# Two set-up blocks of a graph kernel made one: the destination list loaded by ScalarE's queue, the table clears begun behind the source keys with a semaphore for each table, and the index lists and three groups' loads moved beside the input stage

## The reference, cut to what matters

```python
xn = _layernorm(x, axis=-1)
# layer 0, twice (the edges come sorted by dst):
msg = ew[:, None] * h[src]
agg = jax.ops.segment_sum(msg, dst, num_segments=x.shape[0])
# layer 1:
edge_proj = edge_attr @ W_sum + b_sum
sum3d = jax.ops.segment_sum(edge_proj, src, num_segments=num_nodes)
```

## Time and profile before

| | us |
|---|---|
| median of 3 runs | 6724.04 (6717.91 to 6748.71) |
| the profiled execution | 6726.44 |
| its span in the trace | 6724.7 |
| mean granted TensorE clock | 0.735 of full speed |
| GpSimd busy, by the page | 4268.7 (63%) |

### The profile page before, as it was taken

How to read it: one execution, slowest core, us unless ns; L and a number is a source line. 1 busy time by engine, 2 the same in 40 slices (tenths; PEclk the granted TensorE clock), 3 DMA queues, 4 the chain that set the end, 5 groups by cost and what they waited for, 6 DMA issues and landing times. The chain is left out here.

```text
span 6724.7 us, 77268 instructions
## 1 busy us (share of the span) xinstructions
PE 3884.2 (58%) x19263; PEld 3286.8 (49%) x19263; DVE 2787.9 (41%) x7801; ACT 2353.9 (35%) x6709; POOL 4268.7 (63%) x3891
## 2 busy tenths in 40 slices
PE   4655555555555555555655229977765645655653
PEld 3555555545445555554444128866544434444442
DVE  5544444444414444444478666535640011101125
ACT  1225555555435555555433113333421111111112
POOL 3886666666676666666678757875546666666632
PEclk8666666676776766777767569989877777777776
DMA  7774232233473332323478637867341111211235
GB/s 208 133 142 141 86 87 86 86 87 86 87 138 86 87 87 85 87 86 87 85 140 164 174 101 160 168 137 214 107 115 28 32 27 43 45 29 43 45 102 177
DMA packets 691306, 690.18 MB, mean 103 GB/s; under 512 B 97322, under 2 KB 609156, under 8 KB 690360
## 3 DMA queue, kind: packets, MB, share of 16 engines
q0 software_dynamic: 244480, 323.25, 23.8%
q1 hardware_dynamic: 433016, 339.78, 16.6%
q10 hardware_dynamic: 13632, 25.14, 1.0%
HBM read 484.11 MB, written 203.71 MB: 102 GB/s over the span
## 5 line engine op out<-in xcount | busy, mean ns | idle before, releaser
L625 POOL DMA_INDIRECT a_msg<-h_d,a_idx x1664 | 1577.9, 948 | 962.4 <-issue 414.1
L671 PE MATMUL a_part<-a_pick,a_msg 128*128 128x128 f32 x6656 | 1351.0, 369 | 1123.7 <-issue 609.5
L671 PEld LDWEIGHTS a_part<-a_pick,a_msg 128*128 128x128 f32 x6656 | 1218.8, 273 | 1241.9 <-issue 1213.8
L397 POOL DMA_INDIRECT sums_d<-ss_total,ss_row_i x784 | 1287.8, 1643 | 423.5 <-issue 282.6
L3413 POOL DMA_INDIRECT es_edge<-gat_rows_d,el_idx x1024 | 986.4, 963 | 490.2 <-issue 288.3
L651 DVE TENSOR_TENSOR acc<-acc,a_part 128x256 f32 x1664 | 700.9, 421 | 1330.8 <-remote 615.3
L2405 PE MATMUL e_yp<-cb_lent 128*128 128x256 f32 (+1 forms) x1568 | 484.1, 462 | 460.9 <-ACTq L2369 259.9
L2405 PEld LDWEIGHTS e_yp<-cb_lent 128*128 128x128 f32 (+1 forms) x1568 | 363.7, 236 | 584.4 <-ACTq L2369 309.8
L2347 DVE TENSOR_TENSOR cb_lent<-e_yp,cb_lent 128x512 f32<-128x512 f32 (+1 forms) x100 | 68.1, 681 | 1361.6 <-DMA y_d<-mg_y 1016.6
L638 DVE TENSOR_SCALAR a_pick<-ramp,conv_rel,conv_weight 128x128 f32<-128x128 f32 x1680 | 589.5, 352 | 101.5 <-issue 73.5
L2367 ACT ACTIVATE cb_lent<-e_hp,e_b1c 128x256 f32<-128x256 f32 (+1 forms) x400 | 155.3, 471 | 1228.7 <-DMA gm_zo<-in_L_gnn_z_out,gm_out_i 995.8
(11 more groups left out here) (517 smaller groups left out, 5884.7 us busy)
## 6 DMA issues: line engine op xcount, KB each, us to landing
ss_key_row<-keys_d SPq DMA_DIRECT2D x98, 512.0 KB
ss_pay<-in_edge_attr SPq DMA_DIRECT2D x97, 512.0 KB
a_msg<-h_d,a_idx POOLq DMA_INDIRECT x1664
experts_d<-cb_lent SPq DMA_DIRECT2D x96, 256.0 KB
es_edge<-gat_rows_d,el_idx POOLq DMA_INDIRECT x1024
cb_lent<-experts_d SPq DMA_DIRECT2D x29, 512.0 KB
y_rows_d<-node_h SPq DMA_DIRECT2D x28, 512.0 KB
e_xs<-y_rows_d SPq DMA_DIRECT2D x56, 256.0 KB
```

What stands on the lines that cost most here:

```text
L397: nc.gpsimd.indirect_dma_start(self.out_d[q], bass.IndirectOffsetOnAxis(ap=self.row_i[n % 4][:, j:j + 1], axis=0), self.total[n % 4][:, j, ...
L625: nc.gpsimd.indirect_dma_start(msg[(h % 2) * K + b][:], None, table, bass.IndirectOffsetOnAxis(ap=idx[h][:, b:b + 1], axis=0)).then_inc(ga ...
L671: mm = nc.tensor.matmul(part[b % BANKS][:, half, :], msg[(h % 2) * K + b][:, half * P:(half + 1) * P], pick[b][:], start=True, stop=True)
```

## The change

`edge_keys` and `conv_steps` are replaced by one class, `EdgeOrder`, whose parts are called from two places.

- `EdgeOrder.set_up` is one block. The destinations are loaded by ScalarE's queue (`load(act, 1)`), source and weights by SyncE's. ScalarE issues the first SET_UP_CLEARS = 14 of the 24 clears once the source keys have been stored. The input stage's parameters are issued here (`StageParams.issue`) and are waited for in the input stage. `sums.set_up` stands behind the copies of the turned keys. Two groups are loaded instead of five; the first is summed and its rows are chosen.
- `input_stage` takes the rest: four clears ahead of ScalarE's first round and two after each of its first three phases; the seven gathers ahead of GpSimd's scatters; key rows and payload of groups 2 to 4 and the far lists behind the first four x; one gathered block a round in rounds 1 to 7 (`make_rel`, `turn`, `copy_out`); the digit lists and the words in rounds 8 to 10.
- `cleared` is one semaphore for each table, and the first scatter to a table waits for the six clears of that table alone.

```diff
+            def load(eng, j):
+                eng.wait_ge(padded, j + 1)
+                eng.dma_start(raw[j][0:full, :], ...).then_inc(loaded[j], 16)
...
+            @block.sync
+            def _(sp):
+                load(sp, 0)
+                load(sp, 2)
+                for j in (0, 1):
+                    sp.wait_ge(made, j + 1)
+                    sp.dma_start(keys_d[:, j, :]...).then_inc(self.stored[j], 16)
+                sp.wait_ge(loaded[2], 32)
+                sp.dma_start(keys_d[:, 2, :]...).then_inc(self.stored[2], 16)
+                sp.wait_ge(none_made, 1)
+                sp.dma_start(self.sort.sorted_d[0:1, :], self.none[:]).then_inc(none_stored, 16)
+                params.issue(sp)
+                sp.wait_ge(self.stored[0], 16)
+                for n in (0, 1):
+                    sums.load(sp, n, n)
+                sp.wait_ge(none_stored, 16)
+
+            @block.scalar
+            def _(act):
+                load(act, 1)
+                act.wait_ge(zeroed, 1)
+                act.wait_ge(self.stored[0], 16)
+                self.clear(act, 0, SET_UP_CLEARS)
+                for half in (0, 1):
+                    sums.evict_half(act, 0, 0, half)
...
@@ EdgeSums.scatter
-            if chunk == 0:
-                pool.wait_ge(self.cleared, 16 * CLEARS * Q)
+            if nth == 0:
+                pool.wait_ge(self.cleared[q], 16 * CLEARS)
...
@@ input_stage, VectorE
-                    if phase == 2 + i:
+                    if phase == 2 + i and g > first:
                         sums.choose_rows(dve, g - 1, g - 1)
+                if phase == 0 and 1 <= n <= NSB:
+                    order.make_rel(dve, n - 1)
+                if phase == 3 and 1 <= n <= NSB:
+                    order.copy_out(dve, n - 1)
+                if (n, phase) == (8, 3):
+                    order.list_dst_digits(dve)
+                if (n, phase) == (9, 3):
+                    order.list_far_digits(dve)
+                if (n, phase) == (10, 3):
+                    order.make_words(dve)
...
@@ input_stage, GpSimd, TensorE, ScalarE
+            order.gather(pool)
             sums.scatter(pool, first - 2, first + IN_GROUPS - 2)
...
+                if phase == 1 and 1 <= n <= NSB:
+                    order.turn(pe, n - 1)
...
+                if n == 0 and phase < 3:
+                    order.clear(act, SET_UP_CLEARS + 4 + 2 * phase, SET_UP_CLEARS + 6 + 2 * phase)
+            order.clear(act, SET_UP_CLEARS, SET_UP_CLEARS + 4)
             over_fours(act, first_root, copy, head_root, relu, beside=serve)
```

More of the change, by code:

```diff
@@ L123, in _, with __init__, issue, wait @@
             nc.vector.tensor_copy(ramp_16[:], ramp_i[:].unsqueeze(2).broadcast_to([P, P, 16]))
[L126 to L138, removed]
+class StageParams:
+    def __init__(self, k, ctx, tag, loads):
+        self.tiles = [ctx.enter_context(k.nc.sbuf_tensor(f"{tag}_{name}", shape, F32)) for name, shape, _ in loads]
+        self.sources = [source for _, _, source in loads]
+        self.loaded = ctx.enter_context(k.semaphore(f"{tag}_params_in"))
+    def issue(self, sp):
+        for t, source in zip(self.tiles, self.sources):
+            sp.dma_start(t[:], source, allow_slow_non_contiguous=True).then_inc(self.loaded, 16)
+    def wait(self, eng):
+        eng.wait_ge(self.loaded, 16 * len(self.tiles))
@@ L139, in sb @@
         def sb(name, shape, dt=F32):
-            return c.enter_context(nc.sbuf_tensor(f"ek_{name}", shape, dt))
+            return c.enter_context(nc.sbuf_tensor(f"eo_{name}", shape, dt))
         def sem(name):
[L143 to L202, removed]
+            return c.enter_context(k.semaphore(f"eo_{name}"))
@@ new lines, in __init__, with bank @@
+        self.first, self.chunk_i = sb("first", [P, NSB]), sb("chunk_i", [P, NSB], I32)
+        self.got = [sb(f"got{b}", [P, 3 * P]) for b in range(NSB)]
+        self.far_in, self.index_made, self.rel_made, self.turned_to, self.copied = map(sem, (
+            "far_in", "index_made", "rel_made", "turned_to", "copied"))
+        self.stored = [sem(f"stored{j}") for j in range(3)]
+        self.gathered = [sem(f"gathered{b}") for b in range(NSB)]
+    def bank(self, c):
+        self.turned = c.enter_context(self.nc.psum_tensor("eo_turned", [P, 4, P], F32))
@@ new lines, in clear, with gather @@
+    def clear(self, act, first, last):
+        run = self.tables[0].shape[0] * self.tables[0].shape[1] // P // CLEARS
+        zero = self.spare.rearrange("p t f -> p (t f)")[:, 0:run]
+        for n in range(first, last):
+            q, part = divmod(n, CLEARS)
+            rows = self.tables[q].rearrange("(p r) f -> p (r f)", p=P)
+            act.dma_start(rows[:, part * run:(part + 1) * run], zero).then_inc(self.cleared[q], 16)
+    def gather(self, pool):
+        table = self.keys_d.rearrange("c j e -> c (j e)")
+        pool.wait_ge(self.index_made, 1)
+        for j in range(3):
+            pool.wait_ge(self.stored[j], 16)
+        for b in range(NSB):
+            self.nc.gpsimd.indirect_dma_start(self.got[b][:], None, table, bass.IndirectOffsetOnAxis(
+                ap=self.chunk_i[:, b:b + 1], axis=0)).then_inc(self.gathered[b], 16)
@@ L1165, in serve @@
                     sums.load(sp, g + 4, g + 4)
-            over_fours_io(sp, load, store, beside=serve)
+            over_fours_io(sp, load, store, beside=serve, behind=order.load_rest)
             all_stored(sp, h_out)
@@ L1352 @@
 CLEARS = 6
+SET_UP_CLEARS = 14
 EARLY_GROUPS = 1
```

356 lines of the change are left out of this document (199 added, 157 removed).

## The result

The changed kernel took 6709.62 us (median of 20 runs, 6693.14 to 6723.36); in the same comparison the kernel before took 6731.96 (20 runs, 6710.90 to 6750.53). The ratio is 0.9969, with an interval of 0.9959 to 0.9980: about 21 us faster, by 14 to 28. The interval lies clear of 1, but the gain is less than half a per cent, so by the bound of the prediction it counts as no change, where "faster" had 0.68. 6709.62 lies 4 us above the range. The profiled execution has a span of 6716.3 us; that of before had 6724.7.

What follows compares the result with a forecast made beforehand. GpSimd's train of scatters was taken to bound the input stage, with a wait-bound set-up ahead of it. Starting the fourth scatter at 86 instead of 126.91 gave 6726.4 - 41 = 6685.4, less 2.4 to the median: 6683 us, range 6660 to 6706.

Steps and rivals of the forecast that it cites:

- step 6: Input stage, last table: head roots end 80.5, issues 81.2, clears land after 5 us; fourth scatter waits from 74 to 86.
- step 7: Scatters after the fourth: it starts 41 us earlier, next rows come in time, 1.96 us a scatter, no more waits than before.
- everything later hangs on that: Stages after the input stage: its end fixes all that follows, so the 41 us gain reaches the program's end.
- step 1: Set-up, list loads: both queues share three DMA engines at 68 GB/s; source and destinations both there at about 18.6, weights 24.3.
- steps 2 and 3: Set-up: VectorE's sums.set_up done at 32.4, step index 36.9; clears start at 26 and run until about 50.
- step 4: First group: key rows end at 51 beside the clears, last eviction 57.3, input stage starts at about 59, bounds 50 and 68.
- step 5: Gathers at the head of GpSimd's input block: 9.5 us, unhidden; first scatter at 68.5 instead of 120.44, at most 52 us gained.
- Step 8: Work moved into the input stage costs nothing: 12.5 us spare a four, under 2.5 us added on VectorE.
- the start is later: Rival, chance 0.22: first key rows and x sit longer behind clears, or second x is late; gain 26 down to 12.
- GpSimd is the only limit: Rival, chance 0.20: clears end sooner or ScalarE's land before 74; gain 52 us, 6664 to 6675.
- does nothing: Rival, chance 0.04: something other than the train of scatters sets the input stage's end; 6724.
- slower: Rival, chance 0.04: the input stage's first ten rounds become the bound as VectorE waits; 37.6 us a four gives 6758.

Runs made afterwards that it cites:

- rows16: Changed kernel with each 111-row list loaded as 96 and 15 rows; 6635.51 us, ratio 0.9921 to the kernel before.
- dst_sp: Changed kernel with the destinations back on SyncE's queue, between source and weights; one execution, 5964.22 us, aggregate stage at 452.99.
- rest_late: Changed kernel with group 4's loads behind the second x and the far lists in round 3; aggregate stage at 457.55 us.
- after_again: Changed kernel, unedited, compared again with the kernel before on chip B; 6658.87 us, ratio 0.9953.
- after_third: Changed kernel, unedited, compared with the kernel before on chip C; 5968.67 us, ratio 0.9941.
- after_fifth: Changed kernel, unedited, compared with the kernel before on chip D; 6658.56 us, ratio 0.9955.
- rows16_again: Repeat on chip D of the changed kernel with lists loaded as 96 and 15 rows; 6635.52 us, ratio 0.9929 to the kernel before.
- rows16_loads: rows16 with sums.set_up behind the casts, loads of groups 0 and 1 ahead of the parameters, clears behind the second payload; 5962.61 us, ratio 0.9929.
- evict_split: rows16_loads with the first group's sums copied after ten of ScalarE's fourteen clears, the other four behind; 6641.33 us, ratio 0.9938.
- delay35: Changed kernel with an idle block of 34 memsets on VectorE between input stage and first aggregate; 6702.86 us, ratio 1.0021 to the kernel before.
- last_first: Changed kernel with all ten remaining clears issued at the head of the input stage; fourth scatter 6.6 us earlier, aggregate stage at 450.95 us.

## Why the prediction was right and wrong

The forecast was a gain of 41 us; measured were 21 by the ratio, 22 by the medians. Three terms make the difference: step 6 (4.0 us), step 7 (2.4), and "everything later hangs on that" (12 to 14).

1. *The lists, step 1.* That both queues use three engines is shown, by rows16, dst_sp and the share of 0.19. What failed is "both at 18.6": the casts at 15.91 and 21.73 lie either side of it, since the destinations' packets began 4 us after their issue. The two queues' shares were even from then on, and the three engines moved 80 GB/s from 11 to 15 us where 68 was taken. The first clear, which hangs on the store of the source keys, was not changed by it.
2. *VectorE and the first clear, steps 2 and 3.* First clear at 25.00, forecast 26. VectorE ran behind by the late destinations: sums.set_up ended at 34.9, forecast 32.4.
3. *The first group, step 4.* Key rows at 51.04, forecast 51; last copy at 57.57, forecast 57.3 for its end; x at 59.12, forecast 59. The first is partly luck: the key rows were asked for 2.5 us late (34.92) and landed in 16.1 us, not 18.6. SyncE's queue had 47 GB/s beside the clears from 41 to 49 us (0.38 MB), not 37.
4. *The gathers, step 5.* 59.71 to 68.75 is 9.0 us, forecast 9.5; first scatter 68.75, forecast 68.5.
5. *The last table, step 6.* x was in at 69.48, forecast 68.3. From there to the end of the head roots (80.50 plus 1.19) it was 12.2, as forecast; the issues ended at 82.29, forecast 81.2. **The term "landing after 5 us" failed**: from there to the scatter at 89.93 it was 7.6. Cost: 2.6 us, beside 1.1 for x. I chose 5, near the best case of 4.0 in the earlier trace rows and far from its median of 10.5. The engines were full again (373 GB/s from 80 to 90 us). Whether SyncE's loads or the clears ahead make the landing long stays open, since rest_late took neither away.
6. *The train, step 7.* From the fourth scatter to the last it was 354.6 us, 352.3 before, with 9.2 us in 19 waits for earlier scatters to land against 7.4 in 12. Over the profiles of each kernel it is 353.6 to 356.4 (five) and 351.7 to 354.6 (three), so "no more waits than before" was off by about 2 us, little more than the spread. Steps 6 and 7 together make the 6.4 us between 41 and 34.6.
7. *"Everything later hangs on that"* **failed in the comparison of the result**: 34.6 us arrived at the aggregate stage and 21 (14 to 28) came out. The other comparisons do not repeat it (gains in us; each start from one profile):

| comparison | earlier at the aggregate stage | faster at the end |
|---|---|---|
| the result | 34.6 | 21 (14 to 28) |
| after_again, B | 33.5 | 31 (22 to 42) |
| after_third, C | 38.5 | 35 (27 to 43) |
| after_fifth, D | 34.4 (against 487.18 of B) | 30 (19 to 41) |
| rows16, B | 45.2 | 53 (44 to 61) |
| rows16_again, D | 42.6 (against 487.18 of B) | 47 (34 to 60) |
| rows16_loads, C | 45.2 | 43 (35 to 51) |
| evict_split, D | 45.2 (against 487.18 of B) | 41 (29 to 54) |
| delay35, B | -9.2 | -14 (-21 to -7) |

   In all but the first the shift of the start lies within the interval of the end: elsewhere a shift at this place reached the end as far as these runs can tell, though a loss of a few us is not excluded (six of the eight ends lie 2 to 5 us short). In the first, 12 to 14 us are missing. With 20 runs on each side the spread of executions does not cover it, and what took them is not known.
8. *Step 8, what moves into the input stage costs nothing*, held within the 2 us of item 6.
9. *Range and chances.* Low and high came from the rivals' starts alone, with the median of one set of three runs as base. In the comparison the kernel before stood at 6731.96 and not 6724.04, 8 us higher, which is more than the 4 us by which the range was missed. The rival "the start is later" is refuted in its start (x at 59.12, not 68) and borne out in part in its other term, the late landing (7.6, between 5 and 10.5); that its gains of 26 down to 12 hold the measured one is luck, for 34.6 arrived at the aggregate stage. "GpSimd is the only limit" is refuted by the wait of 15.78; "does nothing" and "slower" by the ratios.

## What to carry to other kernels

Follow a load from its shape to the number of DMA engines before moving it to another queue: here the second queue brought nothing, and two pieces instead of one brought 10 us. When the DMA engines are full, a transfer that is issued earlier takes its time from another: the wait at the end travels along (rows16), or shows up at the loads (last_first) or at x (evict_split). An engine that issues many transfers in a row also delays its own compute behind them, but moving the copies ahead (evict_split) did not bring the next scatter earlier. Read a gain of half a per cent both in the stage where it arises, where times repeat within 4 us, and at the end with many runs; one profile cannot tell it there, and here the two did not agree in one comparison of four.

## What the runs showed of the hardware

- One kernel, the same program, took 6732, 6688 and 6003 us in different comparisons, with a mean granted clock of TensorE of 0.735, 0.740 and 0.776. Its input stage, paced by DMA and GpSimd, hardly changed: the aggregate stage of before starts at 486.92, 487.18 and 490.46.
- An engine that issues many DMAs in a row is held by them: fourteen clears of 537.5 KB kept ScalarE's queue for 17.85 us, 1.3 us each, against 0.4 us each for the last two, which were issued five us behind the pair before them with the engines just as full (373 GB/s).
- Two queues that use the same three engines bring no more bandwidth (a share of 0.19 with one list moving and with two) and take turns evenly by packets: 46 and 43 from 11 to 15 us. With packets of unequal size the bytes are uneven: from 41 to 49 us 748 packets of the clears carried 2.87 MB and 750 of SyncE's queue 0.38 MB.
- On ScalarE's queue the first packet of the destinations moved about 4 us after the issue (from 6.83 to between 10.5 and 11.5 us, in five profiles), while the source's, on SyncE's queue, had moved by 7.5 us, asked for at 5.89. Why is not known.
